# Leaky ReLU moved from VectorE into ScalarE's copy out of PSUM, and the loop over images written out

## The reference

```python
x = _L0_conv_ref(x, ...)   # 1x1 convs, softmax attention of each 32x32 channel map, batch norm, + x
x = _L1_conv_ref(x, ...)   # group norm, 8-head self-attention over 1024 pixels, projection, + x
x = _L2_conv_ref(x, ...)   # group norm, linear attention, group norm, exact gelu, 1x1 conv, + xn
x = _L3_conv_ref(x, ...)
# _L3_conv_ref:
out = input + bias[None, :, None, None]
out = _sep_upfirdn(out, upf, UP, 1, UP_PAD)               # 12 taps, 32x32 -> 64x64
out = jax.nn.leaky_relu(out, NEG_SLOPE) * FLRELU_SCALE    # slope 0.2
out = _sep_upfirdn(out, down_filter, 1, DOWN, DOWN_PAD)   # 64x64 -> 32x32
```

## Time and profile before

| what | value |
|---|---|
| median of 3 runs | 3870.22 us (3865.36 to 3873.83) |
| profiled execution: time, and span between its first and last instruction | 3865.28 us, 3863.4 us |
| TensorE busy, share of the span | 3622.2 us, 94% |
| VectorE busy | 2890.1 us, 75% |
| ScalarE busy | 2972.7 us, 77% |
| mean granted TensorE clock, share of full speed | 0.957 |
| image 0 / images 1 to 14 each / image 15's period and everything behind it | 190.3 / 229.2 to 234.1 / 313.7 us |

### The profile page before, as it was taken

How to read it: one execution, slowest core, us unless ns; L and a number is a source line. 1 busy time by engine, 2 the same in 40 slices (tenths; PEclk the granted TensorE clock), 3 DMA queues, 4 the chain that set the end, 5 groups by cost and what they waited for, 6 DMA issues and landing times.

```text
span 3863.4 us, 72651 instructions
## 1 busy us (share of the span) xinstructions
PE 3622.2 (94%) x22401; PEld 1790.8 (46%) x22401; DVE 2890.1 (75%) x5019; ACT 2972.7 (77%) x6992; POOL 41.3 (1%) x57
## 2 busy tenths in 40 slices
PE   6989999999999999999999999999999999999987
PEld 3444545354453544545354453544545354453423
DVE  4667778778777777778778787777778778787755
ACT  2888878878787887878878787887878878788852
POOL 0000000000000000000000000000000000000000
PEclk7889999999999999999999999999999999999998
DMA  2212120121211112120121211112120121211100
GB/s 76 58 39 61 40 70 7 51 59 39 72 35 37 45 42 67 40 70 7 50 59 40 72 30 42 45 42 67 40 70 7 51 59 40 72 30 41 34 17 11
DMA packets 75657, 177.20 MB, mean 46 GB/s; under 512 B 16352, under 2 KB 19040, under 8 KB 73184
## 3 DMA queue, kind: packets, MB, share of 16 engines
q1 hardware_dynamic: 74656, 170.38, 16.2%
q10 hardware_dynamic: 576, 1.57, 0.2%
HBM read 36.62 MB, written 17.30 MB: 14 GB/s over the span
## 4 chain that ended last, share of the span: by engine, by line
PE 80%; issue 7%; DVE 7%; ACT 6%; SPq 0%; ACTq 0%; DMA 0%; DVEq 0%; POOL 0%; POOLq 0%
PE ps L1102 29%; PE ps L1167 12%; PE ps L1130 12%; PE ps L1146 10%; PE ps L1718 3%; ACT ps L986 3%; PE ps L1768 2%; DVE mxh L680 2%; PE ps L1653 2%; PE ps L1750 2%; PE ps L1760 2%; PE ps L1665 2%; PE ps L1777 2%; DVE k L819 1%; ACT u L1048 1%
## 5 line engine op out<-in xcount | busy, mean ns | idle before, releaser
L986 ACT ACTIVATE ps<-ps,mxh 128x512 f32<-128x512 f32 x2048 | 1365.8, 674 | 196.3 <-DVE mxh L680 169.2
L680 DVE TENSOR_REDUCE mxh<-ps 128x1 f32<-128x512 f32 x2048 | 1309.9, 679 | 273.9 <-PE ps L1146 266.1
L977 ACT ACTIVATE prob<-ps 128x512 f32<-128x512 f32 x2048 | 1122.0, 611 | 354.2 <-PE ps L1130 347.3
L1130 PE MATMUL ps<-qs,ks 97*128 97x512 f32 x2048 | 892.6, 513 | 38.3 <-issue 29.1
L1146 PE MATMUL ps<-ks,qs 96*128 96x512 f32 x2048 | 703.1, 419 | 33.3 <-ACT ps L986 18.3
L1130 PEld LDWEIGHTS ps<-qs,ks 97*128 97x128 f32 x2048 | 353.9, 195 | 603.9 <-issue 356.2
L1167 PE MATMUL ps<-prob,vo 128*32 128x512 f32 x4096 | 580.2, 640 | 0.0
L1146 PEld LDWEIGHTS ps<-ks,qs 96*128 96x128 f32 x2048 | 404.1, 197 | 179.9 <-ACT ps L986 79.2
L986 ACT ACTIVATION_READ_ACCUMULATOR ps<-ps,mxh 128x1 f32 x2048 | 443.2, 216 | 0.0
L1102 PE MATMUL ps<-xn,wqk 128*128 128x512 f32 x512 | 246.1, 614 | 13.3 <-DVE lo L663 9.3
L1102 PE MATMUL ps<-wkv,xn 128*128 128x512 f32 x512 | 244.5, 607 | 3.7 <-DVE xn L607 3.7
(11 more groups left out here) (121 smaller groups left out, 3576.8 us busy)
## 6 DMA issues: line engine op xcount, KB each, us to landing
qs<-hi SPq DMA_DIRECT2D x256, 128.0 KB, 2.3
ks<-hi SPq DMA_DIRECT2D x248, 128.0 KB, 2.3
xb<-in_x SPq DMA_DIRECT2D x32, 512.0 KB, 4.3
qs<-lo SPq DMA_DIRECT2D x128, 128.0 KB, 2.3
xa<-xb SPq DMA_DIRECT2D x16, 1024.0 KB, 4.6
recs<-recd SPq DMA_DIRECT2D x64, 256.0 KB
out<-xn SPq DMA_DIRECT2D x32, 512.0 KB, 2.6
ks<-lo SPq DMA_DIRECT2D x124, 128.0 KB, 2.3
```

The lines of the kernel that those rows point to most:

```text
L680: dve.tensor_reduce(mxh[:, k, e:e + 1], ps[:, MAX_BANKS[at % 3], :], AX_X, ALU.max, negate=True).then_inc(max_ok.sem, 1)
L977: act.activation(prob[:, n % 2, h, :], ps[:, k % 2, :], ACT.Exp).then_inc(p_ok.sem, 1)
L986: act.activation(ps[:, bank, :], ps[:, bank, :], ACT.Exp, bias=mxh[:, k, e:e + 1], accum_out=sumh[:, m // NT % 2, k, e:e + 1]).then_inc(su ...
L1130: pe.matmul(ps[:, k % 2, :], ks[0:STACK + 1, (u // 2) * Q4 + h, s * P:(s + 1) * P], qs[0:STACK + 1, u, h, :], start=True, stop=True).then_ ...
```

## The change

The slope is applied while ScalarE copies out of PSUM: the function `Copy` becomes `Prelu` with alpha 0.2. The VectorE function `leaky`, its eight names in `SIDE` and `TAIL` and the semaphore `u2_ok` go; TensorE's `short` waits for `u2_in` instead. Second, `periods` calls the period's code once for each of the images 1 to 15 with plain numbers. The loop, its branches, the registers of `copied` and the register form of `Signal` go on all five engines; every wait is for a constant. No other step is moved, and the banks are the same.

```diff
-    45: ["wu00"], 46: ["wu01"], 47: ["hu00", "rows3"], 48: ["leaky00", "hu01"], 49: ["hu02", "leaky01", "zt1"],
...
+    45: ["wu00"], 46: ["wu01"], 47: ["hu00", "rows3"], 48: ["hu01"], 49: ["hu02", "zt1"],
...
     def __call__(self, image, k):
-        image, away = image if isinstance(image, tuple) else (image, 0)
-        return image * (self.per_image * self.size) + ((away * self.per_image + k) * self.size + START)
...
+        return (image * self.per_image + k) * self.size + START
...
-        def periods(eng, first, period, last):
+        def periods(first, period, last):
 
             first()
             period(0, None, 1)
-            with eng.Fori(1, B - 1) as b:
-                period((b, 0), (b, -1), (b, 1))
-            period(B - 1, B - 2, None)
+            for b in range(1, B):
+                period(b, b - 1, b + 1 if b < B - 1 else None)
             last(B - 1)
...
-            def leaky(i, ct, q):
-
-                dve.wait_ge(u2_in.sem, u2_in(i, 4 * ct + q + 1))
-                tile = u2[:, q // 2, q % 2, :, :].rearrange("p a n -> p (a n)")
-                dve.scalar_tensor_tensor(out=tile, in0=tile, scalar=SLOPE, in1=tile,
-                                         op0=ALU.mult, op1=ALU.max).then_inc(u2_ok.sem, 1)
...
-                    act.activation(u2[:, q // 2, q % 2, :, :].rearrange("p a n -> p (a n)"), both(bank_of(name, i)), ACT.Copy)                        .then_inc(u2_in.sem, 1)
+                    act.activation(u2[:, q // 2, q % 2, :, :].rearrange("p a n -> p (a n)"), both(bank_of(name, i)), ACT.Prelu,
+                                   alpha=SLOPE).then_inc(u2_in.sem, 1)
...
             def short(i, ct, half, p):
 
-                pe.wait_ge(u2_ok.sem, u2_ok(i, 4 * ct + 2 * half + p + 1))
+                pe.wait_ge(u2_in.sem, u2_in(i, 4 * ct + 2 * half + p + 1))
```

More of the change, by code:

```diff
@@ L127, in __call__ @@
     def __call__(self, image, k):
-        image, away = image if isinstance(image, tuple) else (image, 0)
-        return image * (self.per_image * self.size) + ((away * self.per_image + k) * self.size + START)
-def number(image):
-    return image[0] + image[1] if isinstance(image, tuple) else image
+        return (image * self.per_image + k) * self.size + START
 def chain_kernel(nc, x, weights, vectors, rows, filters, consts, recd, out):
@@ L334, in chain_kernel @@
         u2_in = signal("u2_in", 8)
-        u2_ok = signal("u2_ok", 8)
         hd_mm = signal("hd_mm", 8)
@@ L348, in chain_kernel @@
         MAX_BANKS = (2, 3, 5)
-        def periods(eng, first, period, last):
+        def periods(first, period, last):
             first()
             period(0, None, 1)
-            with eng.Fori(1, B - 1) as b:
-                period((b, 0), (b, -1), (b, 1))
-            period(B - 1, B - 2, None)
+            for b in range(1, B):
+                period(b, b - 1, b + 1 if b < B - 1 else None)
             last(B - 1)
-        def copied(eng, n, *images):
-            if n % 4 or not isinstance(images[0], tuple):
-                return images
-            register = eng.alloc_register(f"image_at_step{n}")
-            eng.reg_mov(register, images[0][0])
-            copy = eng.snap(register, min_val=1, max_val=B - 2)
-            return [(copy, away) for _, away in images]
         def turn_at(n):
@@ L379, in load @@
                 for ct in range(CT):
-                    sp.dma_start(xb[:, ct, :], x[number(j), ct * P:(ct + 1) * P, :]).then_inc(x_in.sem, 16)
+                    sp.dma_start(xb[:, ct, :], x[j, ct * P:(ct + 1) * P, :]).then_inc(x_in.sem, 16)
             def copy_x(b, i, j):
@@ L429, in store @@
                 sp.wait_ge(o3_ok.sem, o3_ok(i, ct + 1))
-                sp.dma_start(out[number(i), ct * P:(ct + 1) * P, :], o3[:, ct, :]).then_inc(stored.sem, 16)
+                sp.dma_start(out[i, ct * P:(ct + 1) * P, :], o3[:, ct, :]).then_inc(stored.sem, 16)
             def side(name, b, i, j):
@@ L464, in period @@
                 for n in range(STEPS):
-                    b, i, j = copied(sp, n, b, i, j)
                     for name in [*beside(2 * n, i, j), *beside(2 * n + 1, i, j)]:
@@ L471, in last @@
                     side(name, None, i, None)
-            periods(sp, first, period, last)
+            periods(first, period, last)
             sp.wait_ge(stored.sem, stored(B, 0))
@@ L505, in period @@
                 for n in range(STEPS):
-                    b, i, j = copied(pool, n, b, i, j)
                     for name in [*beside(2 * n, i, j), *beside(2 * n + 1, i, j)]:
@@ L512, in last @@
                     side(name, None, i, None)
-            periods(pool, first, period, last)
+            periods(first, period, last)
         @block.vector
@@ L911, in side @@
                     wide_turned(i, int(name[2]), digit)
-                elif name.startswith("leaky"):
-                    leaky(i, int(name[5]), digit)
                 elif name.startswith("hd"):
@@ L936, in period @@
                 for n in range(STEPS):
-                    b, i, j = copied(dve, n, b, i, j)
                     t = turn_at(n)
@@ L958, in last @@
                     side(name, None, i, None)
-            periods(dve, first, period, last)
+            periods(first, period, last)
         @block.scalar
@@ L1073, in period @@
                 for n in range(STEPS):
-                    b, i, j = copied(act, n, b, i, j)
                     for pair in range(2):
@@ L1090, in last @@
                     side(name, None, i, None)
-            periods(act, first, period, last)
+            periods(first, period, last)
         @block.tensor
@@ L1853, in period @@
                 for n in range(STEPS):
-                    b, i, j = copied(pe, n, b, i, j)
                     for pair in range(2):
@@ L1871, in last @@
                     side(name, None, i, None)
-            periods(pe, first, period, last)
+            periods(first, period, last)
 def kernel(x, **w):
```

## The result

The changed kernel takes **3776.1 us** at the median (3769.9 to 3782.0, four runs), the kernel before 3871.3 beside it (3865.4 to 3873.8, four runs). The ratio is 0.9756, with a 95% interval of 0.9735 to 0.9777: 2.4% faster, 95 us. The forecast was 3815 us, the range began at 3790. The direction was right and the gain, 95 us, was nearly twice the 52 that I had worked out. The profiled execution took 3773.3 us (span 3771.1); that of before took 3865.3.

The account below looks back on a forecast made before the run. TensorE was taken as the bound, busy 222.5 of 231.8 us in image 1. Terms 26.3 + 15 + 6 + 1.5 + 3.6 = 52.4 us off 3865.3 gave 3812.9, 3817.8 on the median; forecast 3815 us, range 3790 to 3842.

Parts of the forecast that it names:

- Term 1: Loop's end: TensorE stands idle 2.0 us at each of 13 taken branches, on the path; 26.3 us gained.
- Rival 4: Branch not the cause: written-out code stands 2.0 us elsewhere in each image; about 3862 us, no difference; chance 0.03.
- Term 2: Steps 0 and 1: the branch's stall brings the lower clock in 10 images, 1.5 us each; 15 us, bounds 0 and 15.
- The step that failed: Steps 30 and 31: lower clocks, some 21 us in all, expected to stay; counted only as the gain's far bound.
- Step 11: Within steps 0 to 22, which the prediction called dense on TensorE, citing steps 3 to 5; no gain foreseen.
- Term 3: Step 30: without register instructions, turn4 and VectorE's copy follow 0.44 us sooner in 14 images; 6 us, bounds 0 and 6.
- Term 4: Leaky passes in the images mostly covered by ScalarE; 0.1 us in step 31 of 15 images, 1.5 us; far bound 18.
- Term 5: Tail: without eight leaky passes TensorE sets the pace; 3.6 us, bounds 2 and 5.3 if last products keep full clock.
- Registers free elsewhere: Register instructions cost nothing where TensorE is dense, hidden by its queue of products, as steps 3 to 5 showed.
- rival 2: Lower clocks of steps 30 and 31 go too, some 20 us more; 3795 us; chance 0.10.

Follow-up runs that it names:

- e2: Kernel before with images written out, no branch or registers, leaky passes kept on VectorE; 3785.9 us, ratio 0.9789.
- e1: Kernel before with loop, branch and registers kept, leaky passes removed and the negative slope left out; 3828.2 us, ratio 0.9905.
- e14: Kernel before, with loop, registers and leaky passes, but the second 128 small products moved half a step later; 3813.7 us, ratio 0.9866.
- e10: Written-out kernel with leaky passes (e2), with the second 128 small products moved half a step later; 3752.9 us, ratio 0.9709.

## Why the prediction was wrong

- **Term 1 (26 us) held.** The changed kernel has no wait of the score product for issue, where the earlier trace rows had 29.1 us, and step 31 takes 8.17 us at full clock, as expected. The pause on GpSimd of nearly the same length stood 25 us at the same edge and cost them all, so a stall there is on the path. The Trainium skill's figure for a compare-and-branch (page Advanced Engine Details and Errata, section Control Flow Timing) is some 108 ns; the one that wasn't taken agrees roughly (83 ns), the taken ones, 3323 to 3910 ns, don't. Rival 4 is out; its 3862 us should have read 3856, 3815 with terms 1 and 2 put back.
- **Term 2 (15 us) held in size, not in cause; that its number came out was luck.** Steps 0 and 1 fell to 14.7 us. But a branch without the passes, and a stall without a branch, left step 0 at full clock in 11 and 12 of 13 images. In most images it needed the stall and more idle time in step 30 as well (10 of 13 before, 6 of 13 with both pauses). That ten lower clocks stood behind thirteen branches, and none behind two crossings without one, showed that the stall is needed. I read it as enough.
- **The step that failed** is the one that left the lower clocks of steps 30 and 31 as they are. I had their price right, 21 us (22 by TensorE's busy time), and held that they would stay, since they come at the loop's exit too, without a branch. That spoke against the branch, not against the registers and the passes, which are in image 14 as well and go with the change. All 22 us went, and 0.34 us of pause put the lower clock back in 8 of 14 images, 12 us of it.
- **Step 11 (13 us) was put at nothing without a row.** The prediction called steps 0 to 22 dense, going by steps 3 to 5. In steps 10 and 11 TensorE stood some 0.8 us for issue and then ran at the lower clock, before and after. Parting the small products shows what that costs; why step 11 is shorter in the changed kernel stays open.
- **Term 3 (6 us) held in size, but not for its reason alone.** `turn4` follows the copy by 0.06 us, as expected (step 30 of image 4):

```profile
1197.52 1.02 ACT L1018 ACTIVATE u<-ps 128x1024 f32<-128x1024 f32 x1
...
1198.60 0.28 PE L1125 MATMUL ps<-ident,stat 128*32 128x128 f32 x1 [0.28 <-ACT u L1018]
1199.33 0.27 DVE L692 COPY srow<-ps 32x128 f32<-32x128 f32 x1
```

  VectorE's copy comes 0.45 us after `turn4`, longer than before (0.31), now behind a maximum that VectorE is still at. At full clock step 30 fell from 7.20 to 6.76 us, the 0.44 of the term. But taking away the registers alone gave 0.25 (e2) and the passes alone 0.32 (e1), so part of it came from the passes, which the term didn't have.
- **Term 4 was too small.** "Covered by ScalarE" was wrong for the pass ahead of step 30: it acted on ScalarE, over VectorE's maximum. The passes cost 38 us in the loop and 7 to 10 in the written-out kernels, against 5 by terms 4 and 5 together. The argument beside it, that as a pass of its own the leaky ReLU belongs on VectorE, isn't borne out in float32 either: 1212 ns there, 1024 for ScalarE's copy.
- **Term 5 (3.6 us) held for the sum, by luck.** From the tail's first `hu`, the last transposition ends 20.1 us later instead of 22.3, 2.2 us closer and not 3.6, and the last product ends 22.2 us later instead of 26.0:

```profile
3744.66 2.85 PE L1730 MATMUL ps<-qe,up_m 64*128 64x512 f32 x12 [1.72 <-DVE qe L784]
...
3761.09 3.64 DVE L792 STREAM_TRANSPOSE k<-ps 128x512 f32<-128x512 f32 x4
...
3764.87 1.94 PE L1747 MATMUL ps<-k,dn_m 128*64 128x512 f32 x8 [1.57 <-DVE k L792]
```

  2.2 us are VectorE's, 1.7 the clock of the last products (1.94 us against 3.63), which I had put into the far bound. The passes make both: the loop without them (e1) has 20.0 and 22.1 us, the written-out kernel with them (e2) 22.2 and 25.8.
- **Registers free elsewhere**: true for steps 3 to 5, which I had looked at the earlier trace rows. Kept without a branch they cost 40 us at the median. Of the 53 between the two profiled executions 43 are TensorE's busy time (3615.2 against 3572.4 us for the same 22401 products), which I read as the lower clock.
- The chances: rival 2 had 0.10, and even its 3795 us left out step 11, for which no row was read.

## What to carry to other kernels

Where TensorE's granted clock falls behind short waits, a few tenths of a microsecond of idle time can cost several times themselves (5 us of pause cost 18 here). So price a lower clock by what stands idle ahead of it, and ask of each part of the change whether it is in every image that shows the dip, before leaving the dip in the sum. A pass that no wait names can still act, by pushing a later instruction on its own engine for which the next one waits: follow the queue behind it, not only its own reader. Long rows of very small products deserve a look of their own: ordinary products between them were worth 33 us here (31 by the ratios), about a third of what the whole change brought, for two lines. And look at such a gap in several images: whether it stays at one product or wanders tells what it belongs to.

## What the runs showed of the hardware

- 0.34 us more idle time in step 30 brought TensorE's clock down in 8 of 14 images (a stretch at 0.81 instead of 1.00), where 1.9 us at the edge, right ahead of dense work, did so in 1 of 13. Length alone doesn't tell whether the clock falls.
- In 256 products of 32 x 32 in a row TensorE stood for issue, 0.5 to 1.3 us in the changed kernel, at a place that comes again every 256 of its recorded instructions: behind the 211th product in each pass of the loop, 17 products earlier from image to image where the images are written out. With 14 ordinary products between the two runs of 128 the gap is gone in all of images 1 to 14 of the loop (e14), and in 12 of 14 written out (e10; 1.03 us stayed in image 2, 0.30 in image 9).
- Register moves of a constant that nobody uses are not in the executed program. A memset on GpSimd of 128 x 256 (0.31 us) or 128 x 2048 (1.8 us) makes a pause that can be seen in the trace.
